# Four graph layers on one core: VectorE's program without register copies and covered waits, sums added four tiles behind their one-hots in six PSUM banks

## The reference

```python
h = relu(layernorm(x));  x = x + L0(src, edge_type_200, dst, h, ...)
h = relu(layernorm(x));  x = x + L1(h, edge_index, ...)
h = relu(layernorm(x));  x = x + L2(h, edge_index, edge_attr_128, ...)
h = relu(layernorm(x));  x = x + L3(h, edge_index, edge_type_2, ...)

# L0: three times  h = tanh((segment_sum(rel_w[rels] * h[tails], heads) + h) @ W)
#     then e = leaky_relu(x@en.T[heads]@u1 + x@en.T[tails]@u3 + rel_term); alpha = softmax(e)
#     out = segment_sum(alpha * x[tails], heads)
# L1: graph attention with 8 heads: softmax of leaky_relu(a_src[src] + a_dst[dst]) within each dst,
#     out = segment_sum(h[src] * alpha, dst) + bias
# L2: relu(x@W_self.T + b + segment_sum(x_nei[src] + edge_attr@w_edge.T, dst) / deg)
# L3: relu(segment_sum(m_data or m_ctrl by edge_type, dst) + X@W_self.T + b)
```

## Time and profile before

| | us |
|---|---|
| runs, median of 3 | 10254.23 (10246.95 to 10256.1) |
| profiled execution, time | 10236.95 |
| its span | 10235.2 |

### The profile page before, as it was taken

How to read it: one execution, slowest core, us unless ns; L and a number is a source line. 1 busy time by engine, 2 the same in 40 slices (tenths; PEclk the granted TensorE clock), 3 DMA queues, 4 the chain that set the end, 5 groups by cost and what they waited for, 6 DMA issues and landing times. The chain is left out here.

```text
span 10235.2 us, 108302 instructions
## 1 busy us (share of the span) xinstructions
PE 6012.9 (59%) x17328; PEld 3631.6 (35%) x17328; DVE 5636.8 (55%) x20801; ACT 1046.0 (10%) x3382; POOL 6471.4 (63%) x6594
## 2 busy tenths in 40 slices
PE   0577056666666666666566665777754555565555
PEld 0455022223333333333233233555543333343333
DVE  7566067776555545554666776666673333343333
ACT  0000000000000000000333332333320000010000
POOL 5777766666666666665666654666645666646666
PEclk9655566767666766666666665555555555565555
DMA  2233111112111121112111121111112111121112
GB/s 41 65 82 91 14 43 45 46 46 54 47 46 47 47 55 46 46 47 55 42 44 44 43 42 45 45 44 45 45 30 61 43 44 43 44 60 46 46 47 56
DMA packets 397664, 491.74 MB, mean 48 GB/s; under 512 B 135634, under 2 KB 302358, under 8 KB 396726
## 3 DMA queue, kind: packets, MB, share of 16 engines
q0 software_dynamic: 208736, 381.82, 15.6%
q1 hardware_dynamic: 185226, 101.57, 3.5%
q10 hardware_dynamic: 3020, 1.36, 0.1%
HBM read 448.73 MB, written 37.86 MB: 48 GB/s over the span
## 5 line engine op out<-in xcount | busy, mean ns | idle before, releaser
L1228 PE MATMUL PS<-OH,RING 128*128 128x128 f32 (+1 forms) x9816 | 3920.9, 529 | 2607.5 <-issue 1044.5
L1228 PEld LDWEIGHTS PS<-OH,RING 128*128 128x128 f32 x9816 | 2304.0, 289 | 4223.1 <-issue 2033.0
L1741 POOL DMA_INDIRECT RING<-TAB,IDX x2418 | 2306.0, 954 | 1217.9 <-issue 640.8
L620 DVE TENSOR_TENSOR RA<-RA,PS 128x256 f32 x2418 | 1006.7, 416 | 1385.5 <-PE PS L1228 683.1
L620 DVE TENSOR_TENSOR RB<-RB,PS 128x128 f32 x2490 | 716.9, 288 | 1381.3 <-PE PS L1228 883.2
L1690 POOL DMA_INDIRECT REC<-RC x800 | 958.3, 1198 | 323.8 <-issue 242.3
L1757 POOL DMA_INDIRECT RING<-TABQ,IDX x806 | 785.1, 974 | 522.5 <-issue 224.3
L1741 POOL DMA_INDIRECT RING<-TABN,IDX x830 | 784.0, 945 | 523.5 <-PE PS L1228 311.8
L1741 POOL DMA_INDIRECT RING<-TABM,IDX x830 | 783.6, 944 | 474.6 <-PE PS L1228 165.1
L608 DVE TENSOR_SCALAR OH<-IOTA,KEY,WE 128x256 f32<-128x256 f32 x2418 | 1025.9, 424 | 80.0 <-ACT RA L1539 48.9
L1320 PE MATMUL PS<-OH,RING 128*128 128x256 f32 x1612 | 750.2, 593 | 403.2 <-ACT OH L1563 225.8
(11 more groups left out here) (367 smaller groups left out, 5239.9 us busy)
## 6 DMA issues: line engine op xcount, KB each, us to landing
RING<-in_edge_attr_dram SPq DMA_DIRECT2D x830, 64.0 KB
RING<-TAB,IDX POOLq DMA_INDIRECT x2418
RING<-TABN,IDX POOLq DMA_INDIRECT x830
RING<-TABM,IDX POOLq DMA_INDIRECT x830
RING<-TABQ,IDX POOLq DMA_INDIRECT x806
REC<-RC POOLq DMA_INDIRECT x800
TAB<-HN SPq DMA_DIRECT2D x18, 512.0 KB, 3.2
RING<-TABG,IDX POOLq DMA_INDIRECT x560
```

Of the source, the lines that this page charges most:

```text
L620: v.tensor_tensor(sl, sl, PS[k % 4][:, 0:width], ALU.add).then_inc(s_ad, 1)
L1228: t_.matmul(PS[t % 4][:, 0:width], GD[:, t % 16, :], OH[:, t % 4, 0:width], start=True, stop=True).then_inc(s_mm, 1)
L1741: p.indirect_dma_start(GD[:, t % 16, :], None, table, bass.IndirectOffsetOnAxis(ap=idx[:, t:t + 1], axis=0)).then_inc(s_ring[t % 16], 16)
```

## The change

The change does four things, the first two also in the passes scores and GAT:

- `window` gives the loaded register itself, from 16 newly named ones for each load, without a copy. The copies go from VectorE and, in GAT, from TensorE.
- Waits of VectorE go or move. In `sum_pass` one-hot t no longer waits for product t-4 but for add t-5 (`s_ad` at t-4), the add that stands just ahead of it in the program, and an add no longer waits for the add before it, except in the last four. In scores and GAT the wait for the add before goes too; one-hots there wait for the add of four tiles back (scores) or, in GAT, for nothing, and the weighting of rows waits for the add of four tiles back and no longer for its rows.
- In `sum_pass` the add follows its one-hot by four tiles and no more by two. The one-hots have eight buffers: `OH` seen as 8 x 128, or for 256 wide ones a part of RB, for which VectorE waits for the store of ATTD before L0a. The products go around six PSUM banks (0, 1, 2, 3, 6, 7), and product t waits for add t-6.
- POOL's gather t in `gathers` waits for product t-12. The ring keeps its 16 slots.

```diff
--- before.py
+++ after.py
@@ -31,6 +31,7 @@
 LAST = E - 128
 SC_BRANCH, SC_FIRST = 88, 128
 GS = 11
+BANKS, ADD_LAG, AHEAD = (0, 1, 2, 3, 6, 7), 4, 12
 NG = -(-NT0 // GS)
 NL1 = 832
 NC1 = NL1 // 16
@@ -232,6 +233,8 @@
         V3R, U3B = RC[:, 5376 + 512:5376 + 640], RC[:, 5376 + 640:5376 + 768]
         RET, V1B = ST[:, 500:628], RC[:, 512:640]
         PB = RB[:, 0:NW * WN]
+        OHN8 = OH[:, :, :].rearrange("p a b -> p (a b)").rearrange("p (a b) -> p a b", b=WD)
+        OHW8 = RB[:, 0:8 * WN].rearrange("p (a b) -> p a b", b=WN)
         S0, QE = SC1, SC2
         MG, FG, ZG = ST[:, 0:80], ST[:, 80:160], ST[:, 160:240]
         GM, SW = ST[:, 240:320], ST[:, 320:352]
@@ -310,10 +313,17 @@
         for k_ in (ATTR, SUM0, SUM0 + 1, SUM0 + 2, MEAN, TYPED):
             before[k_] = sum(ROW_PASSES[i] for i in before)
 
+        used = []
+
         def window(e, regs, tab, t, n=NW):
+
             if t % 16 == 0:
-                e.load(regs, tab[0:1, t:t + 16])
-            return e.snap(regs[t % 16], min_val=0, max_val=n - 1)
+                for r in regs:
+                    e.free_register(r)
+                used.append(t)
+                regs[:] = [e.alloc_register(f"w_{len(used)}_{i}") for i in range(16)]
+                e.load(regs, tab[0:1, t:t + 16], bass_reorder=False)
+            return e.snap(regs[t % 16], donate=True, min_val=0, max_val=n - 1)
 
         block = ctx.enter_context(nc.Block())
 
@@ -591,8 +601,8 @@
 
             def sum_pass(i, acc, tab, key, weighted=False, choose=False, own_terms=False):
                 n, base = ROW_PASSES[i], before[i]
-                width, blocks = (WN, NW) if weighted else (WD, ND)
-                for t in range(n + 2):
+                width, blocks, oh = (WN, NW, OHW8) if weighted else (WD, ND, OHN8)
+                for t in range(n + ADD_LAG):
                     if t < n:
                         if own_terms:
                             own_term(t)
@@ -602,22 +612,22 @@
                             if t + 1 < n:
                                 wsel(t + 1)
                             v.wait_ge(s_wsel, t + 1)
-                        if t >= 4:
-                            v.wait_ge(s_mm, base + t - 3)
+                        if t > ADD_LAG:
+                            v.wait_ge(s_ad, base + t - ADD_LAG)
                         if weighted:
-                            v.tensor_scalar(OH[:, t % 4, :], IOTA[:, :], key[:, t:t + 1], WE0[:, t:t + 1], ALU.is_equal,
+                            v.tensor_scalar(oh[:, t % 8, :], IOTA[:, :], key[:, t:t + 1], WE0[:, t:t + 1], ALU.is_equal,
                                             ALU.mult).then_inc(s_oh, 1)
                         else:
-                            v.tensor_scalar(OH[:, t % 4, 0:WD], IOTA[:, 0:WD], key[:, t:t + 1], None,
+                            v.tensor_scalar(oh[:, t % 8, :], IOTA[:, 0:WD], key[:, t:t + 1], None,
                                             ALU.is_equal).then_inc(s_oh, 1)
-                    if t >= 2:
-                        k = t - 2
+                    if t >= ADD_LAG:
+                        k = t - ADD_LAG
                         w = window(v, regs, tab, k, blocks)
+                        if t >= n:
+                            v.wait_ge(s_ad, base + k)
                         v.wait_ge(s_mm, base + k + 1)
-                        if k:
-                            v.wait_ge(s_ad, base + k)
                         sl = acc[:, bass.ds(w * width, width)]
-                        v.tensor_tensor(sl, sl, PS[k % 4][:, 0:width], ALU.add).then_inc(s_ad, 1)
+                        v.tensor_tensor(sl, sl, PS[BANKS[k % 6]][:, 0:width], ALU.add).then_inc(s_ad, 1)
                 v.wait_ge(s_ad, base + n)
 
 
@@ -687,6 +697,7 @@
 
 
             v.wait_ge(s_te, 13)
+            v.wait_ge(s_attd, 16)
             for layer in range(3):
                 if layer:
                     v.wait_ge(s_acc, 13 * layer)
@@ -795,17 +806,18 @@
                 a = t - LAG0
                 if 0 <= a < NT0:
                     if a >= 4:
-                        v.wait_ge(s_oh0, a - 3)
+                        v.wait_ge(s_ad0, a - 3)
                     v.tensor_scalar(OHB[:, a % 4, :], IOTAB[:, :], KEY0[:, a:a + 1], None, ALU.is_equal).then_inc(s_ohb, 1)
                 a = t - LAG0 - 3
                 if 0 <= a < NT0:
                     w = window(v, regs2, WTAB0, a)
                     sl = ACC[:, bass.ds(w * WN, WN)]
-                    v.wait_ge(s_mm0, a + 1)
-                    if a:
+                    if a and a + 3 >= NT0:
                         v.wait_ge(s_ad0, a)
                     if a % GS == 0:
                         v.wait_ge(s_fac, a // GS + 1)
+                    v.wait_ge(s_mm0, a + 1)
+                    if a % GS == 0:
                         v.scalar_tensor_tensor(out=sl, in0=sl, scalar=FG[:, a // GS:a // GS + 1], in1=PS[a % 4][:, 0:WN],
                                                op0=ALU.mult, op1=ALU.add).then_inc(s_ad0, 1)
                     else:
@@ -1011,16 +1023,15 @@
 
             for t in range(NL1 + LAG1 + 3):
                 if t < NL1:
-                    if t >= 51:
-                        v.wait_ge(s_tp, t - 50)
-                        v.wait_ge(s_ox, t - 50)
                     v.tensor_scalar(OBR[:, t % 51, 0:WD], IOTAB[:, 0:WD], KEY1[:, t:t + 1], None, ALU.is_equal).then_inc(s_ob, 1)
                 chain_part(t, 0)
                 a = t - LAG1 + 1
                 if 0 <= a < NL1:
                     rows = rows_of(a)
-                    landed(v, GAT, a)
-                    v.wait_ge(s_ca, 8 * (a // 16) + 7)
+                    if a % 16 == 0:
+                        v.wait_ge(s_ca, 8 * (a // 16) + 7)
+                    if a > 3:
+                        v.wait_ge(s_ab, a - 3)
                     v.tensor_tensor(
                         rows[:, 0:128].rearrange("p (h c) -> p h c", c=16), rows[:, 0:128].rearrange("p (h c) -> p h c", c=16),
                         rows[:, 128:136].unsqueeze(2).to_broadcast([128, 8, 16]), ALU.mult).then_inc(s_gx, 1)
@@ -1034,9 +1045,9 @@
                     else:
                         w = window(v, regs, WTAB1, a, ND)
                     sl = RB[:, bass.ds(w * 146, 146)]
+                    if a + 4 > NL1:
+                        v.wait_ge(s_ab, a)
                     v.wait_ge(s_mb, a + 1)
-                    if a:
-                        v.wait_ge(s_ab, a)
                     v.tensor_tensor(sl, sl, PS[a % 3][:, 0:146], ALU.add).then_inc(s_ab, 1)
                 chain_part(t, 2)
             own_done(chain)
@@ -1211,7 +1222,7 @@
 
             def sum_pass(i, own_terms=False):
                 n, base = ROW_PASSES[i], before[i]
-                width = WN if SUM0 <= i < SCORES else WD
+                width, oh = (WN, OHW8) if SUM0 <= i < SCORES else (WD, OHN8)
                 for t in range(n):
                     if own_terms and t % 16 == 8 and t // 16 < NT:
                         k = t // 16
@@ -1223,9 +1234,9 @@
                         t_.matmul(PS[5][:, 0:128], ONES[0:1, :], ROWS[0:1, 0:128], start=False, stop=True).then_inc(s_own_t, 1)
                     t_.wait_ge(s_oh, base + t + 1)
                     landed(t_, i, t)
-                    if t >= 4:
-                        t_.wait_ge(s_ad, base + t - 3)
-                    t_.matmul(PS[t % 4][:, 0:width], GD[:, t % 16, :], OH[:, t % 4, 0:width], start=True, stop=True).then_inc(s_mm, 1)
+                    if t >= 6:
+                        t_.wait_ge(s_ad, base + t - 5)
+                    t_.matmul(PS[BANKS[t % 6]][:, 0:width], GD[:, t % 16, :], oh[:, t % 8, :], start=True, stop=True).then_inc(s_mm, 1)
 
             def all_added(i):
                 t_.wait_ge(s_ad, before[i] + ROW_PASSES[i])
@@ -1736,8 +1747,8 @@
 
                 n, base = ROW_PASSES[i], before[i]
                 for t in range(n):
-                    if t >= 6:
-                        p.wait_ge(s_mm, base + t - 5)
+                    if t >= AHEAD:
+                        p.wait_ge(s_mm, base + t - AHEAD + 1)
                     p.indirect_dma_start(GD[:, t % 16, :], None, table,
                                          bass.IndirectOffsetOnAxis(ap=idx[:, t:t + 1], axis=0)).then_inc(s_ring[t % 16], 16)
```

## The result

The changed kernel takes 10108.33 us (median of 4 runs, 10106.53 to 10114.49) and the kernel before 10252.59 beside it (10246.95 to 10256.1): a ratio of 0.9863, 95% interval 0.9848 to 0.9878. It is faster by 144 us (1.4%), not by the 770 that were forecast. The profiled execution took 10109.49, its span is 10107.7.

What follows compares the result with a forecast made beforehand. POOL, standing still for late products, was taken to bound the gather passes. Savings of 110 + 270 + 205 + 140 + 20 + 25 = 770 from 10236.95 gave 9467, with 17 us more called 9,485; range 9,390 to 9,920.

Steps and rivals of the forecast that it cites:

- POOL's step of 1.245 us: Gather passes: POOL needs 0.94 us for a gather and 0.30 before the next; idle time beyond, 807.3 us, awaits products.
- The pauses of TensorE: Gather passes: TensorE's products come in bursts with pauses of about 5 us between, which make POOL lose time.
- MEAN's 10.07 us at an own term: MEAN: VectorE idles 10.07 us at the own term's three products, and POOL then starts its gather 4.91 us late.
- Twelve tiles of lead: Gather passes: POOL twelve tiles ahead, not six, feels only stalls above 14.9 us; 725 us saved with the change's other parts.
- The copies: VectorE: 7350 register copies at a median of 36 ns, 265 us over eight passes, with no saving of their own counted.
- Scores: Scores pass: POOL's lead there stays as it was; bounds −10 and 235, 20 us saved.
- GAT: GAT pass: number and lead of products stay as before; bounds −10 and 240, 25 us saved.
- ATTR: ATTR, 690 us, lies beside POOL's scatters, for which VectorE idles 255.99 us; making it faster gains nothing.
- TensorE has a pace of its own of 1.43 us: Rival: TensorE or landing rows limit tiles to 1.43 us; MEAN gains 75 us, the last two passes 45; 10,134, chance 0.08.
- bursts of 0.73 us: L0c: after a pause, adds come 0.73 us apart, taken as a sign that TensorE catches up with ease.
- The slower rival: Rival: VectorE without gaps slows POOL's gathers to 1.19 us, 999 us more less the 770; 10,483, chance 0.04.
- Half of the gather term given back: Rival: a faster POOL brings more TensorE pauses, so only 362 of the gather passes' 725 us stay; 9,847, chance 0.15.

Runs made afterwards that it cites:

- experiment 3: Changed kernel, L0b with gathers alone, L0c with VectorE's loop uncoupled, TYPED adding into eight places in turn: L0b 1101 us, TYPED 1.416 us a tile.
- experiment 4: Changed kernel with free gathers beside one VectorE or TensorE loop per pass, against the same loops without gathers: one-hots 1.400 us each, products 5.600 (0.547 without).
- experiment 1: Changed kernel with products doubled, halved or left out: 1.438, 1.415, 1.413 us a tile; TYPED without gathers or with plain loads: 0.585.
- experiment 6: Changed kernel with free full-size gathers beside VectorE loops, signals thinned or without operations, POOL clearing columns in L0b and L0c: L0b one-hots 0.56 us each, TYPED signals 1.392.

## Why the prediction was wrong

- **POOL's step of 1.245 us** failed, and the rest hangs on it. The prediction put it as "fixed when it need not wait: a gather of 0.94 us and 0.30 us before the next", and took all beyond as waits for late products, 807 us. The rows are right but are those of a stretch of few gathers. In the long run a gather costs 1.40 us on such a chip, alone or not. L0b's gathers with nothing to wait for took 1101 us in experiment 3, the first 180 of them at 1.25, and 1148.8 in the kernel before: what could be won there was at most 47 us, and by the long-run step (806 × 1.40 = 1128) 20, not the 135 of the forecast. The waits for products that the 807 us were added up from are how that pace shows in POOL's rows, not what makes it; without any product the step was still 1.413.
- **The pauses of TensorE** The earlier trace rows were read as its own bursts. Its products were late because their completions had to take turns with gathers: 5.60 us for one alone, in experiment 4. MEAN's 10.07 us at an own term would be three products more in that queue, which no run tested. I noted that the end of a matmul is modelled, and didn't ask why it should end late.
- **Twelve tiles of lead** were to be worth most of 725 us. They are worth nothing (0.9999 in the kernel before, and no loss when the changed kernel goes without them): a lead covers a stall, not a rate. My check, that the longest wait is shorter than the new lead, tested only the former.
- **The copies** were priced at nothing in the gather passes. They were worth 1.15% alone where completions queue and 0.12% where they don't. I took the median of 36 ns from the row and passed over its maximum of 1398, which is 1.40 again.
- **Scores** 20, measured 56. The old waits alone leave 1197.6 us there, and the copies put back cost 28 (1238.3 for 1210.7), so the copies are half of it as far as is shown; **GAT** 25, measured −3, within its bounds.
- **ATTR** hidden: right, 47 us shorter between its adds and 303.1 us of idle time ahead of line 535.
- **Rivals.** "TensorE has a pace of its own of 1.43 us" gave 10,134 and the measured time is 10,108. Its number was right to 0.3%, MEAN's part to 2 us, and it named the landing of rows beside TensorE; but a pace of TensorE is refuted by experiment 1, and its 45 us for "the two last passes" were in fact 56 of scores and −3 of GAT, so the closeness is luck in part. I held ATTR and the bursts of 0.73 us against it. ATTR was no witness: its rows come by SP's plain loads, and the scatters beside it start every 1.60 us (958.3 us busy and 323.8 idle for 800, on the page of the kernel before). That three passes with products of two widths shared 1.43 us was the best evidence in the profile, and I gave it 0.08. The slower rival had a gather go to over 1.13 us; it went to 1.095 in free gathers, not in the kernel (946 ns), and not through VectorE. Half of the gather term given back gave 9,847 and missed by 261 us: nothing was given back, as there was nothing to take.

What stays open: what it is that gathers and completions share; how the copies, and in MEAN both parts, bring their gain; and why two chips haven't got the limit. No chip came up in two groups of the experiments, so it may as well be something of the hour as of the chip. Every run here was recorded by the profiler, and one-hots that signal nothing have turns like the others, so the recording itself may be what is shared. Whether the limit, and with it most of the 144 us, is there without recording wasn't tried.

## What to carry to other kernels

When passes with different work per tile share one pace, ask first which instruction they have in common, and measure it with nothing waiting for it for a thousand of its kind; a step read between two waits is the best case, not the rate. A longer lead helps only against stalls, and it is cheap to test alone. Where POOL issues indirect DMAs without a break, count the operations and signals of the other engines too, and try what their register copies cost: a median of 36 ns didn't tell. And before explaining a ratio, look whether the kernel it is measured against takes the same time on the next chip.

## What the runs showed of the hardware that was not expected

- An indirect DMA on POOL takes 1.25 us for some 180 in a row and 1.40 us after; the 1.40 is the same at 128 rows of 512 bytes, 128 rows of 8 bytes and 32 rows of 512; on two chips it stayed at 1.25 (128 rows of 512 bytes, TYPED of experiment 6).
- Beside them VectorE completes one operation per 1.40 us (0.249 to 0.389 otherwise), signalling or not, and TensorE one product per 5.60 us (0.547 otherwise). Address computations and register loads had no turn of their own (32 turns for 16 tiles). At one gather per 1.68 us a one-hot takes 0.56 us.
- The same kernel took 8988 us on one chip, 8981 on a second and 10235 to 10400 on others, steadily within each group of runs.
